# Attention products packed from three to two a head, with a copy and an addition after them

## What is computed

```python
q = (x @ Wq + bq); k = (y @ Wk + bk); v = (y @ Wv + bv)      # 16 heads of 16
attn = softmax(q k^T / 4)                                    # per head, 256 x 77
out = attn @ v
x = x + tanh(g_xattn) * (relu(out @ W1 + b1) @ W2 + b2)      # x normalised before
comb = top-2 weights of the 8 experts from softmax(max(xn @ gate_W + gate_b, 1e-4))
x = x + tanh(g_ffn) * sum_e(comb_e * (xn @ expert_W[e] + expert_b[e])) / 2
```

## Time and profile before

| what | value |
|---|---|
| time, median of 3 runs | 954.12 us (953.99 to 955.93) |
| profiled execution, own time | 955.33 us |
| its span | 953.5 us |
| TensorE busy | 919.9 us, 96% |
| VectorE busy | 809.1 us, 85% |
| ScalarE busy | 719.6 us, 75% |
| GpSimd busy | 633.1 us, 66% |

### The profile page before, as it was taken

How to read it: one execution, slowest core, us unless ns; L and a number is a source line. 1 busy time by engine, 2 the same in 40 slices (tenths; PEclk the granted TensorE clock), 3 DMA queues, 4 the chain that set the end, 5 groups by cost and what they waited for, 6 DMA issues and landing times.

```text
span 953.5 us, 26162 instructions
## 1 busy us (share of the span) xinstructions
PE 919.9 (96%) x9410; PEld 669.3 (70%) x9410; DVE 809.1 (85%) x2108; ACT 719.6 (75%) x1517; POOL 633.1 (66%) x793
## 2 busy tenths in 40 slices
PE   4789999999999999999999999999999999999997
PEld 2566777777777777777777777777777777777763
DVE  5776988888988888898888889888888988888876
ACT  4756878877787877778787777778777878877661
POOL 5545776667677666767766767866676776667643
PEclk8578999999999999999999999999999999999999
DMA  6100000000000000000000000000000000000000
GB/s 206 29 15 1 27 27 16 26 26 19 21 26 25 17 27 26 13 27 27 15 26 26 26 13 26 27 15 27 26 26 13 27 26 16 26 13 13 13 13 23
DMA packets 17615, 24.61 MB, mean 26 GB/s; under 512 B 2814, under 2 KB 9168, under 8 KB 17488
## 3 DMA queue, kind: packets, MB, share of 16 engines
q1 hardware_dynamic: 17488, 22.94, 7.7%
HBM read 14.54 MB, written 8.39 MB: 24 GB/s over the span
## 4 chain that ended last, share of the span: by engine, by line
PE 91%; issue 3%; DVE 2%; POOL 2%; ACT 1%; POOLq 0%; DVEq 0%; ACTq 0%
PE e L755 33%; PE g L755 19%; PE t L939 9%; PE t L804 6%; PE s L890 4%; PE g L956 3%; PE s L827 3%; PE s L828 3%; PE s L826 2%; PE g L764 2%; PE g L901 2%; PE g L966 1%; PE t L924 1%; PE g L845 1%; PE g L836 1%
## 5 line engine op out<-in xcount | busy, mean ns | idle before, releaser
L381 POOL TENSOR_TENSOR p_lo<-p_f,p_hi 77x512 f16<-77x512 f32 x161 | 187.8, 1182 | 82.8 <-ACT p_hi L570 82.8
L755 PE MATMUL e<-we_hi,x2T_lo 128*128 128x512 f16 x496 | 189.4, 382 | 0.0
L755 PE MATMUL e<-we_lo,x2T_hi 128*128 128x512 f16 x496 | 189.1, 381 | 0.0
L755 PE MATMUL e<-we_hi,x2T_hi 128*128 128x512 f16 x496 | 188.9, 381 | 0.0
L1233 DVE SCALAR_TENSOR_TENSOR acc<-e,comb,acc 128x256 f32<-128x256 f32 x307 | 146.6, 478 | 27.4 <-PE e L755 24.0
L569 ACT ACTIVATE p_f<-t 77x512 f32<-77x512 f32 x256 | 152.3, 595 | 15.5 <-PE t L804 8.6
L570 ACT ACTIVATE p_hi<-t 77x512 f16<-77x512 f32 x256 | 152.2, 595 | 0.0
L1283 DVE TENSOR_REDUCE row_max<-s 128x6 f32<-128x462 f32 (+1 forms) x192 | 108.0, 577 | 7.6 <-PE s L890 5.2
L365 POOL TENSOR_TENSOR ve<-mv,ln_eps 128x1 f32<-128x1 f32 x64 | 14.6, 227 | 141.8 <-DVE mv L1334 141.8
L826 PE MATMUL s<-v_hi,p_lo 77*128 77x17 f16 x1024 | 98.1, 172 | 5.2 <-POOL p_lo L381 5.1
L826 PEld LDWEIGHTS s<-v_hi,p_lo 77*128 77x128 f16 x1024 | 84.1, 97 | 25.4 <-issue 10.6
(11 more groups left out here) (195 smaller groups left out, 2859.8 us busy)
## 6 DMA issues: line engine op xcount, KB each, us to landing
x_sb<-in_x SPq DMA_DIRECT2D x32, 256.0 KB, 2.7
out<-acc SPq DMA_DIRECT2D x31, 256.0 KB, 2.0
we_f<-in_L_ffn_expert_W SPq DMA_DIRECT2D x2, 1024.0 KB, 9.6
y_sb<-in_ctx SPq DMA_DIRECT2D x32, 57.8 KB
w_f<-in_L_xattn_W SPq DMA_DIRECT2D x2, 512.0 KB, 7.3
wq_f<-in_L_xattn_Wq SPq DMA_DIRECT2D x1, 256.0 KB, 4.1
out<-acc SPq DMA_DIRECT2D x2, 128.0 KB, 1.7
wkv_f<-in_L_xattn_Wk SPq DMA_DIRECT2D x1, 192.0 KB, 2.9
```

The costliest lines, as they stand in the source:

```text
L381: pool.tensor_tensor(p_lo[:, r].rearrange("m h n -> m (h n)"), p_f[:, r, :], p_hi[:, r].rearrange("m h n -> m (h n)"), ALU.subtract).then_ ...
L755: mm = pe.matmul(out_ap, a, c, start=(first and i == 0), stop=(last and i == n - 1))
```

## The change

`v_hi` and `v_lo` become one tensor `v_both` with 33 columns a head: 16 high parts, the 1, 16 low parts. One product of `p_hi` and one of `p_lo` with all 33 columns take the place of the three of 17. The bank then holds, for each of 15 of its 16 pairs of half and head, 33 columns (`PACK`), of which the last 16 are still to be added to the first 16. For that, ScalarE copies the last 16 of each of the 15 to SBUF (`low_values_copy`, 128x240), and VectorE adds them (`add_low_values`). The sixteenth pair (16 x 33 columns would not fit in 512) keeps three products. The two copies a step stand in ScalarE's order around `q_stack_high`, the two additions ahead of `reciprocals`.

The low part of group 6 goes from GpSimd to VectorE, and that of 7 from VectorE to GpSimd, in the first attended row too, where GpSimd made both. GpSimd makes both key blocks ahead of `stack_comb`. On TensorE `combT_transposes` goes behind expert product 1, and both `expert_biases` behind `key_stack_transposes`. In step 32 (s == B) product 6 is made ahead of the second group's `attend` in place of after `scores(m, 6)`, and product 5 of the next step is made at the end of this one.

```diff
+PACK = DV + DH
+PACKED = T * H // 2 - 1
-POOL_LOW = (1, 3, 4, 5, 6)
-VECTOR_LOW = (0, 2, 7)
-FIRST_LOW = 7
+POOL_LOW = (1, 3, 4, 5, 7)
+VECTOR_LOW = (0, 2, 6)
...
-                pool.tensor_copy(v_hi[:, u, :, 0:DH], v).then_inc(v_split, 1)
+                pool.tensor_copy(v_both[:, u, :, 0:DH], v).then_inc(v_split, 1)
                 pool.wait_ge(v_split, 2 * b + 1)
-                pool.tensor_tensor(v_lo[:, u, :, 0:DH], v, v_hi[:, u, :, 0:DH], ALU.subtract).then_inc(v_split, 1)
+                pool.tensor_tensor(v_both[:, u, :, DV:PACK], v, v_both[:, u, :, 0:DH], ALU.subtract).then_inc(v_split, 1)
...
                 if has(s, 0):
                     key_blocks(b, 0)
+                if has(s, 0):
+                    key_blocks(b, 1)
                 if has(s, -2):
                     stack_comb(e, eu)
                 if has(s, 0):
-                    key_blocks(b, 1)
                     k_low(b)
...
+            def low_values_copy(b, half):
+                act.wait_ge(av_done, 8 * b + 4 * half + 4)
+                at_least(act, low_values_added, 2 * (b - 1) + half + 1)
+                parts = S[half][:, 0:PACKED * PACK].rearrange("p (a d) -> p a d", d=PACK)
+                act.activation(low_values[:, half], parts[:, :, DV:PACK], ACT.Copy).then_inc(low_values_copied, 1)
...
                 if front:
                     highT_copies(b)
+                if mid:
+                    low_values_copy(m, 0)
+                if front:
                     q_stack_high(b)
+                if mid:
+                    low_values_copy(m, 1)
+                if front:
                     k_stack_high(b)
...
                     for t in range(T):
-                        at = (t * (H // 2) + h % (H // 2)) * DV
+                        a = t * (H // 2) + h % (H // 2)
                         hi, lo = p_hi[:, r, e, t * P:(t + 1) * P], p_lo[:, r, e, t * P:(t + 1) * P]
-                        dst = S[half][:, at:at + DV]
-                        pe.matmul(dst, lo, v_hi[:, u, h, :], start=True, stop=False)
-                        pe.matmul(dst, hi, v_lo[:, u, h, :], start=False, stop=False)
-                        mm = pe.matmul(dst, hi, v_hi[:, u, h, :], start=False, stop=True)
+                        if a < PACKED:
+                            dst = S[half][:, a * PACK:(a + 1) * PACK]
+                            pe.matmul(dst, hi, v_both[:, u, h, :], start=True, stop=False)
+                            mm = pe.matmul(dst, lo, v_both[:, u, h, :], start=False, stop=True)
+                        else:
+                            dst = S[half][:, a * PACK:a * PACK + DV]
+                            pe.matmul(dst, lo, v_both[:, u, h, 0:DV], start=True, stop=False)
+                            pe.matmul(dst[:, 0:DH], hi, v_both[:, u, h, DV:PACK], start=False, stop=False)
+                            mm = pe.matmul(dst, hi, v_both[:, u, h, 0:DV], start=False, stop=True)
...
                 if mid:
                     output_transposes(m)
-                if first and s <= B:
-                    combT_transposes(e, eu)
                 if front:
                     scores_for_max(b, 1)
                 if first and s <= B:
                     experts(e, eu, 1, s - 2)
-                    expert_biases(e, 0)
+                    combT_transposes(e, eu)
                 if front:
                     scores_for_max(b, 2)
-                if first and s <= B:
-                    expert_biases(e, 1)
...
                 if front:
                     key_stack_transposes(b)
+                if first and s <= B:
+                    expert_biases(e, 0)
+                    expert_biases(e, 1)
...
+            def add_low_values(b, half):
+
+                dve.wait_ge(low_values_copied, 2 * b + half + 1)
+                parts = S[half][:, 0:PACKED * PACK].rearrange("p (a d) -> p a d", d=PACK)
+                dve.tensor_tensor(parts[:, :, 0:DH], parts[:, :, 0:DH], low_values[:, half], ALU.add).then_inc(low_values_added, 1)
...
             def normalise(b, half, t):
                 if t == 0:
                     dve.wait_ge(rden_done, 2 * b + half + 1)
+                    dve.wait_ge(low_values_added, 2 * b + half + 1)
...
                 if first:
                     gate(e, eu, 12)
+                if mid:
+                    p_low(m, 6)
                 if last:
                     add_expert(f_pair, f, fu, 6, 0, s - 3)
...
-                if mid and m > 0:
-                    p_low(m, 7)
-                if mid:
+                if mid:
+                    add_low_values(m, 0)
                     reciprocals(m, 0)
                     normalise(m, 0, 0)
                     normalise(m, 0, 1)
                 if mid:
+                    add_low_values(m, 1)
                     reciprocals(m, 1)
```

More of the change, by code:

```diff
@@ L140, in gated_block @@
         rden = sb("rden", [P, 2, T, H // 2])
+        low_values = sb("low_values", [P, 2, PACKED, DH])
         o = sb("o", [P, T, D])
@@ L466, in step @@
                         p_low(m, g)
-                if has(s, -1) and m == 0:
-                    p_low(m, FIRST_LOW)
                 if has(s, 0):
                     key_blocks(b, 0)
+                if has(s, 0):
+                    key_blocks(b, 1)
                 if has(s, -2):
@@ L812, in attend @@
                     pe.wait_ge(max_taken, 6 * b + 6)
[L813 to L816 removed]
+                if g in VECTOR_LOW:
+                    pe.wait_ge(p_lo_vector, len(VECTOR_LOW) * b + VECTOR_LOW.index(g) + 1)
                 else:
[L818 removed]
+                    pe.wait_ge(p_lo_pool, len(POOL_LOW) * b + POOL_LOW.index(g) + 1)
                 r, half = g % RING, g // 4
@@ L1002, in step @@
                     power_spread()
-                if last and s <= B + 1:
+                if last and s <= B:
                     experts(f, fu, 5, s - 3, (lambda: transposes_y(pair, b, u)) if front else None)
@@ L1019, in step @@
                     scores(m, 3)
+                if s == B:
+                    experts(f, fu, 6, s - 3)
+                if mid:
                     attend(m, mu, 1)
@@ L1029, in step @@
                     scores(m, 6)
-                if last:
+                if last and s != B:
                     experts(f, fu, 6, s - 3)
@@ L1099, in step @@
                     experts(e, eu, 4, s - 2)
+                if s == B:
+                    experts(e, eu, 5, s - 2)
                 if mid:
```

22 lines of the change are left out of this document (9 added, 13 removed).

## The result

| | before | the change |
|---|---|---|
| median of 4 runs | 954.27 us (953.99 to 955.93) | 967.78 us (967.67 to 970.31) |
| span of the profiled execution | 953.5 us | 966.0 us |
| one step (period) | 27.93 us | 28.38 us |

A forecast was written before the change was run, and what follows sets the result against it. TensorE, 96% busy, bounds the second half of a step; in the first, other engines' chains do. Outputs' chain +0.07, transposes +0.22 and biases' wait +0.21 make +0.50 us a step, 968 us; range 944 to 1000.

The forecast's parts named there:

- What TensorE saves: Attention products: 33 columns cost 0.0255 us each, like 17; thirty products fewer save 0.765 us a step.
- The last exponential: ScalarE, first half of a step: its last exponential ends about 0.35 us earlier.
- Low part 7: GpSimd, first half: takes 1.14 us in place of VectorE's 0.74; TensorE waits 0.3 us before the last group.
- The outputs' chain: Copy, additions, reciprocal and products before the outputs' transposes: TensorE waits 0.6 us; expert product 1 starts +0.07 us later.
- The second half: TensorE from expert product 1 on: +0.22 us for comb_stack's moved transposes, +0.21 us waiting ahead of mlp_up.
- the biases' wait: TensorE ahead of mlp_up: biases' products need ScalarE's copy of combT, 0.85 us with 0.64 covered; +0.21 us.
- The sum: All terms of a step together: +0.50 us, over 29 steps +14.5 us, giving 968 us.
- Faster: Rival: outputs' chain hidden if shorter than 1.5 us; -0.32 us a step, 945 us, or 930 at full saving; chance 0.15.
- No change: Rival: additions take 0.25 us and the biases' wait is half; within 0.2% of before; chance 0.08.
- Dearer products: Rival: 33-column products cost 0.036 us, TensorE saves nothing; +0.85 us a step, 979 us; chance 0.50 shared with the forecast.
- The collision: Rival: GpSimd's low part delays VectorE's copy of q; +1.0 to +1.4 us a step, 985 to 995 us; chance 0.27.
- the rival's second stage: VectorE's low part 6 also blocked by GpSimd's low part 7 and key block; +3.1 us a step, 1044 us; within 0.27.

The follow-up runs named there:

- run 9: The change with low part 7 back on VectorE, 6 on GpSimd, and GpSimd's stack_comb ahead of both key blocks; 972.56 us.
- run 12: The change with the kernel before's order on TensorE, and stack_comb between low part 7 and the key blocks on GpSimd; 958.67 us.
- run 5: Kernel before with both halves packed, stack_comb ahead of both key blocks, first attended row and last steps as in the change; 955.38 us.
- run 7: The change with expert products 5 and 6 of the last two steps where they were before; 966.81 us.
- run 10: The kernel before, unpacked, with only GpSimd's stack_comb moved ahead of both key blocks; 954.22 us.
- run 1: The kernel before with only the change's order on TensorE and GpSimd, nothing packed; 960.56 us.
- run 6: The change with low part 7 back on VectorE and 6 on GpSimd, its order on TensorE and GpSimd kept; 1043.02 us.
- run 8: The change with VectorE's copy of q to half precision moved two instructions later; 988.32 us.

## Why the prediction was right

**What TensorE saves.** Right: 0.0255 us at 33 columns. The trace agrees with the rule that the prediction cites there, from the Trainium skill ("TensorE: Matmul & The Clock Gate", Back-to-back issue gap), about 25 ns. One sign missed: TensorE's share was to fall to 93%, and is 95%. A product of 33 columns counts as busy for 0.18 us though the next can start after 0.0255, so the first part of a wait behind one doesn't show in the share.

**The last exponential** ends 0.32 us sooner (0.35 forecast). **Low part 7** is 1.16 us on GpSimd (1.14), and ends at 502.88; TensorE waits for it 0.1 us and not 0.3, since it gets there later than I counted: the wait of 0.24 us for VectorE's sum, ahead of product 7 of row s-3, is not in the prediction. In the change's order low part 7 costs nothing, for run 9 without it has the same 28.37; in the old order it costs 0.19 (run 12 against run 5).

**The outputs' chain.** The mechanism is right, the size a little too large. The copy takes 0.38 us and not 0.46, and `q_stack` starts 0.25 us behind the first one, not 0.36. `o` is complete at 13.59, where the sum had 501.43 - 487.67 = 13.76, and product 1 starts 0.09 us before its old time and not 0.07 after it. TensorE stands about 0.3 us ahead of the outputs' transposes, since it arrives there later than in my sum (13.35, not 13.23), and 0.2 more ahead of product 1, for VectorE's sums. The 0.60 beside the weight load is that engine's own idle time; a matmul's wait is read from the starts. The additions are 0.42 us open and 0.32 from start to start (0.35).

**The second half.** +0.52 (0.43 forecast): 0.22 for the transposes of `comb_stack` and 0.21 for the biases' wait, both to the hundredth, and of the rest 0.07 is a term that I had missed: two biases' products one behind the other take 0.34 us, and spread between other products 0.27.

**The sum.** -0.09 + 0.52 is 0.43 a step against 0.50, 0.44 by the openings. The 2 us that this makes over 29 steps came back at the end, which I had at nothing; the move in step 32 that I had looked at explains 0.8 of them (run 7), and the rest stays open. The start, where I had -0.5, gave 2.7 back, and that was no term of the change. So the direction and the size of a step come from the mechanism, but that the total meets 968 to less than 1 us is luck.

**What the runs say of the causes.** Packing with everything that it needs is -0.07 in the typical step (run 5 against before), of which -0.02 may be the stack's place (run 10). From there TensorE's order alone is +0.51 (run 9 against run 5), and the swap of low parts 6 and 7, with the stack behind the key blocks, then 0.00 (the change against run 9). Taken the other way round the swap alone is +0.19 (run 12 against run 5), since GpSimd's second key block then ends at 14.50 and not at 14.29 and TensorE waits for it, and the order with the stack's place +0.32 (the change against run 12). So the two are not additive: each hides part of the other, and the order costs 0.3 to 0.5. In an unpacked kernel the same order costs 0.18 (run 1), for TensorE uses the time that the transposes leave. So what the prediction says of the second half, that the transposes "no longer fill time before it, where TensorE now waits anyway", was the main term, and not the outputs' chain, to which I gave most of the text.

Nor does the chain alone make the saving of 0.77 us shrink to 0.07. When TensorE reaches the outputs' transposes in the change, it is only 0.32 us ahead of the kernel before (13.35 against 13.67): 0.24 has gone ahead of product 7 of row s-3, where it waits for VectorE's sum, and 0.10 for low part 7. The chain then takes about 0.3. The order was not forced on the packed kernel; run 12 has the change without it, 9 us faster.

**The rivals.** "Faster" fell by its own condition: from the end of the last group's products at 503.17 the chain takes 1.73 us to `o`, and the work that covers it 1.49. (The prediction has 1.85 for the chain; its own times, 501.43 less 499.44, make it 1.99.) "No change" could not have come of its condition, since the prediction's own lower bound, with no wait ahead of the biases at all, is +4 us or 0.4%. "Dearer products" fell with the spacing. The collision was close: `q_hi` began at 499.65, and two low parts of 1.14 after 497.42 end at 499.70. Runs 6 and 8 show what such a collision costs when it comes. That run 6 measured 1043, where the rival's second stage has 1044, is chance: it is another kernel, the low part that stands is VectorE's 7 and not 6, the copy of `q` isn't held up, and a typical step is 2.76 us longer than before, where the rival had 3.1.

**Open.** By what GpSimd and VectorE are told apart when both want the turn. In the kernel before and in run 1, VectorE's low part 7 asks 0.15 to 0.16 us before GpSimd's key block begins and wins; in run 6, with the same distance, it loses. No run here separates the two. By the Trainium skill ("SBUF — State Buffer", Who interferes with whom) the order of issue decides who blocks; the records' order of start, at least, does not decide it here.

## What to carry to other kernels

Ahead of a saving on the busiest engine, follow it to every place where it waits for another engine: here 0.77 us of matmuls shrank to 0.07, partly since it arrives early and waits for a sum that is no earlier, partly since the copy and addition that the packing needs lie between the last group and the output. Packed only where its chain is covered, the kernel kept slightly more (0.11). And a reordering has two prices, what it uncovers where the instruction arrives and what it leaves where it was; the second is a gain only while the engine has nothing to wait for there.

## What had not been expected of the hardware

VectorE and GpSimd take turns by whole instructions where VectorE's operation is a copy from float32 to float16 or reads two tensors from SBUF. Usually the loser stands for one instruction: 0.44 us for the stack or the key block, 0.47 for the copy of `q`. But GpSimd with its next instruction ready can keep the turn: VectorE stood for 2.46 us through two key blocks (run 6), and 3.4 us through three instructions (4.09 less 0.68, run 8). The same program also loses a turn in one of the 28 steps compared and not in the others: once through three instructions in run 8, twice through a single one in runs 5 and 9, worth 1.7 to 4 us a time. What makes that step different isn't shown. A short instruction in float32 of GpSimd between its long ones let VectorE in (run 9, and in the steady steps of run 5).
